# A decoder layer on one core: the second group's feed-forward tokens turned by the DMA queue

## What is computed

```python
def reference(x, ctx_2048, mask_BxS2_bk0, ...):
    x = x + _L0_attn_ref(_layernorm(x, axis=-1), ...)
    x = x + _L0_xattn_ref(_layernorm(x, axis=-1), ctx_2048, mask_BxS2_bk0)
    x = x + _L0_ffn_ref(_layernorm(x, axis=-1), ...)
    return x

def _quantized_matmul(x, w, scale):
    wq = w.astype(jnp.float8_e4m3fn).astype(x.dtype)
    return jnp.einsum('bsi,io->bso', x, wq) * scale

# feed-forward: gate = silu(q(x, gate_w)); up = q(x, up_w); q(gate * up, down_w)
```

## Time and profile before

| | us |
|---|---|
| median of 3 runs | 546.43 (546.37 to 546.47) |
| the profiled execution | 546.76 |
| its span, first to last instruction | 545.0 |

### The profile page before, as it was taken

How to read it: one execution, slowest core, us unless ns; L and a number is a source line. 1 busy time by engine, 2 the same in 40 slices (tenths; PEclk the granted TensorE clock), 3 DMA queues, 4 the chain that set the end, 5 groups by cost and what they waited for, 6 DMA issues and landing times.

```text
span 545.0 us, 10146 instructions
## 1 busy us (share of the span) xinstructions
PE 538.2 (99%) x3936; PEld 424.2 (78%) x3936; DVE 375.1 (69%) x717; ACT 283.1 (52%) x510; POOL 290.3 (53%) x262
## 2 busy tenths in 40 slices
PE   8999999999999999999999999999999999999997
PEld 7877888878888888888888888766686667866676
DVE  6999886888665886659898987355944668344422
ACT  5857886977767786776653442034501344023310
POOL 5398798985783657877795348034400343013320
PEclk9999999999999999999999999999999999999999
DMA  8951222273215310239563712100071001600001
GB/s 291 342 212 65 77 81 78 79 228 123 75 44 161 111 59 2 79 109 299 187 238 101 266 32 103 41 1 0 0 155 38 1 0 27 149 20 0 1 20 59
DMA packets 56176, 53.91 MB, mean 99 GB/s; under 512 B 15168, under 2 KB 37952, under 8 KB 56128
## 3 DMA queue, kind: packets, MB, share of 16 engines
q1 hardware_dynamic: 56128, 53.25, 31.0%
HBM read 36.46 MB, written 13.63 MB: 92 GB/s over the span
## 4 chain that ended last, share of the span: by engine, by line
PE 82%; POOL 10%; DVE 5%; issue 2%; ACT 0%; POOLq 0%; DVEq 0%
PE bank L312 33%; PE bank L506 24%; PE bank L526 15%; POOL q_w L828 2%; POOL q_w L826 2%; POOL probs L819 2%; POOL x_res L842 2%; PE bank L307 2%; PE bank L440 2%; PE bank L450 1%; PE bank L409 1%; DVE q_m L1363 1%; PE bank L361 1%; PE bank L537 1%; PE bank L556 1%
## 5 line engine op out<-in xcount | busy, mean ns | idle before, releaser
L312 PE MATMUL bank<-reduced 128*128 128x512 f32 x936 | 223.3, 394 | 0.3 <-DVE ctxT L1307 0.3
L312 PEld LDWEIGHTS bank<-reduced 128*128 128x128 f32 x936 | 172.8, 188 | 38.2 <-issue 1.1
L934 POOL TENSOR_TENSOR f_parts<-fused,f_parts 128x512 fp32r<-128x512 f32 x48 | 62.9, 1310 | 154.3 <-ACT f_parts L1206 154.3
L1188 ACT ACTIVATE tanh_g<-bank,half_gate 128x512 f32<-128x512 f32 x48 | 33.0, 687 | 141.8 <-PE bank L506 133.0
L526 PE MATMUL bank<-reduced,f_parts 128*128 128x512 f32 x360 | 83.5, 392 | 0.0
L526 PEld LDWEIGHTS bank<-reduced,f_parts 128*128 128x128 f32 x360 | 67.4, 188 | 14.2
L506 PE MATMUL bank<-reduced 128*128 128x512 f32 x288 | 72.1, 402 | 0.0
L1552 DVE SCALAR_TENSOR_TENSOR silu<-tanh_g,bank 128x512 f32<-128x512 f32 x48 | 32.9, 685 | 56.8 <-ACT tanh_g L1188 56.8
L506 PEld LDWEIGHTS bank<-reduced 128*128 128x128 f32 x288 | 54.1, 188 | 12.9
L826 POOL TENSOR_TENSOR q_w<-q_w,q_m 128x512 f32<-128x512 f32 x36 | 49.7, 1381 | 7.8 <-DVE q_m L1365 7.8
L819 POOL TENSOR_SCALAR_AFFINE_SELECT probs<-probs 128x1024 f32<-128x1024 f32 x32 | 37.0, 1161 | 31.0 <-ACT probs L1001 31.0
(11 more groups left out here) (135 smaller groups left out, 761.9 us busy)
## 6 DMA issues: line engine op xcount, KB each, us to landing
quantized<-q_w SPq DMA_DIRECT2D x36, 256.0 KB, 3.4
reduced<-quantized SPq DMA_DIRECT2D x12, 512.0 KB, 6.8
memT_sb<-in_memT SPq DMA_DIRECT2D x16, 256.0 KB, 4.9
mem_sb<-in_mem SPq DMA_DIRECT2D x16, 256.0 KB, 5.9
out<-y_sb SPq DMA_DIRECT2D x15, 256.0 KB, 2.1
q_w<-in_gate_w SPq DMA_DIRECT2D x12, 256.0 KB, 3.5
q_w<-in_up_w SPq DMA_DIRECT2D x12, 256.0 KB, 3.2
x_res<-in_x SPq DMA_DIRECT2D x3, 1024.0 KB, 8.9
```

What stands on the lines that cost most here:

```text
L312: ins = pe.matmul(dst, stationary, moving, start=(n == 0), stop=(n == len(pairs) - 1))
L934: pool.tensor_tensor(f_lo[:, f, :], fused[:, f % 2, :], f_hi[:, f, :].bitcast(F32), ALU.subtract).then_inc(f_lo_ready, 1)
```

## The change

Group 1 now goes the way of groups 2 and 3. `turn_x3`, `x3_high` and `x3_low` are gone. The planes of group 1 lie where `tanh_g` and `silu2` lie, which become one tile `gate_parts`; so the first plane waits until the last `fuse` of group 0 is done with them, and `gate(1, 0)` waits until the planes are turned. On SP the four token tiles of group 1 are turned first, each as soon as it is made, and the planes after them, all in front of the store of token 0; for groups 2 and 3 the planes stay first. `gate_up` waits for `x16` in front of the first half and for `cT_lo` only in front of the low half. In the lists of ACT and DVE the new steps stand around the last cross attention steps.

```diff
+            gate_parts = sb("gate_parts", [P, 4 * TG], F32, ffn)
+            tanh_g = gate_parts[:, 0:2 * TG].rearrange("p (n s) -> p n s", n=2)
+            silu2 = gate_parts[:, 2 * TG:].rearrange("p (n s) -> p n s", n=2)
...
             def gate_up(g, f, banks):
-                if f == 0:
+                if f == 0 and g == 0:
                     for i in range(GT):
-                        if g < 2:
-                            wait_drained(pe, ("N", G, i) if g == 0 else ("T3", g, i))
-                    if g >= 2:
-                        pe.wait_ge(x16_turned, 16 * GT * (g - 1))
-                        pe.wait_ge(x3_lo_made, GT * (g - 1))
+                        wait_drained(pe, ("N", G, i))
+                if f == 0 and g:
+                    pe.wait_ge(x16_turned, 16 * GT * g)
...
                 for n, high in enumerate((f % 2 == 0, f % 2 == 1)):
+                    if f == 0 and not high:
+                        pe.wait_ge(x3_lo_made, GT * g)
...
                     cross(G - 1, 6)
-                    for i in range(GT):
-                        turn_x3(1, i, (4, 3, 1, 7)[i])
                     down(0, 0, 0, DOWN_FIRST)
...
-            def turn_tokens(g):
-
-                sp.wait_ge(last_plane_made, GT * (g - 1))
+            def turn_planes(g):
+                sp.wait_ge(last_plane_made, GT * g)
                 sp.dma_start_transpose(out=planes_T.rearrange("p (n s) -> p n s", s=S),
                                        in_=planes(g).rearrange("p i w d -> p (i w d)")).then_inc(planes_turned, 16)
-                sp.wait_ge(x16_tok_made, GT * (g - 1))
+
+            def turn_tokens(g):
+
+                if g > 1:
+                    turn_planes(g)
                 wait_filled(sp, ("U", g - 1, FT - 1))
                 for i in range(GT):
+                    sp.wait_ge(x16_tok_made, GT * (g - 1) + i + 1)
                     sp.dma_start_transpose(out=x16[:, :, i * S:(i + 1) * S], in_=x16_tok[:, i, :]).then_inc(x16_turned, 16)
+                if g == 1:
+                    turn_planes(g)
 
             for t in range(B - 1):
-                if t in (GT, 2 * GT):
+                if t in (0, GT, 2 * GT):
                     turn_tokens(t // GT + 1)
...
             def gate(g, f):
                 src = wait_filled(act, ("G", g, f))
+                if (g, f) == (1, 0):
+                    act.wait_ge(planes_turned, 16)
...
             cross_second(*step[FT - 1])
+            for i in range(2):
+                token_high(1, i)
             cross(G - 1, 5)
-            x3_high(1)
+            for i in range(2, GT):
+                token_high(1, i)
+            for i in range(GT):
+                token_plane(1, i)
...
             cross(G - 1, 5)
+            for i in range(GT):
+                token_rest(1, i)
             cross(G - 1, 6)
-            x3_low(1)
-            y_out(0)
+            for i in range(GT):
+                token_last_plane(1, i)
+            y_out(0, range(2))
+            planes_low(1)
+            y_out(0, range(2, GT))
```

More of the change, by code:

```diff
@@ L191, in build @@
         with ffn:
-            tanh_g = sb("tanh_g", [P, 2, TG], F32, ffn)
-            silu2 = sb("silu2", [P, 2, TG], F32, ffn)
+            gate_parts = sb("gate_parts", [P, 4 * TG], F32, ffn)
+            tanh_g = gate_parts[:, 0:2 * TG].rearrange("p (n s) -> p n s", n=2)
+            silu2 = gate_parts[:, 2 * TG:].rearrange("p (n s) -> p n s", n=2)
             fused = sb("fused", [P, 2, TG], F32, ffn)
@@ L204, in planes @@
         def planes(g):
-            return x_res[:, GT * (g - 2):GT * (g - 1), :].rearrange("p i d -> p (i d)").bitcast(BF16)\
-                .rearrange("p (i w d) -> p i w d", i=GT, w=2)
+            place = gate_parts[:] if g == 1 else x_res[:, GT * (g - 2):GT * (g - 1), :].rearrange("p i d -> p (i d)")
+            return place.bitcast(BF16).rearrange("p (i w d) -> p i w d", i=GT, w=2)
         planes_T = xn2[:].rearrange("p i d -> p (i d)").bitcast(BF16)
@@ L247, in build @@
         down_loaded, down_late_loaded, down_c_loaded = sem("down_loaded"), sem("down_late_loaded"), sem("down_c_loaded")
-        x3_hi_ready, tanh_ready, f_hi_ready, f_lo_ready = (
-            sem("x3_hi_ready"), sem("tanh_ready"), sem("f_hi_ready"), sem("f_lo_ready"))
+        tanh_ready, f_hi_ready, f_lo_ready = sem("tanh_ready"), sem("f_hi_ready"), sem("f_lo_ready")
         w16_made = sem("w16_made")
@@ L508, in gate_up @@
                             ins.then_inc(done, 1)
[L510 to L513, removed]
             def down(g, i, b, first=0, last=FT):
@@ L1163, in _ @@
                     flag_slabs(slabs_at(FLAGGED, g, 3))
[L1165 to L1169, removed]
             def token_high(g, i):
@@ L1174, in token_high @@
                     wait_filled(act, ("WO", G - 1, GT - 1))
-                    if g > 2:
-                        act.wait_ge(x16_turned, 16 * GT * (g - 2))
+                    if g > 1:
+                        act.wait_ge(x16_turned, 16 * GT * (g - 1))
                 act.activation(x16_tok[:, i, :], xn2[:, i, :], ACT.Copy).then_inc(x16_tok_made, 1)
             def token_plane(g, i):
-                act.wait_ge(rest_made, GT * (g - 2) + i + 1)
-                if i == 0:
+                act.wait_ge(rest_made, GT * (g - 1) + i + 1)
+                if i == 0 and g == 1:
+                    wait_drained(act, ("U", 0, FT - 1))
+                elif i == 0:
                     act.wait_ge(y_ready, GT * (g - 1))
@@ L1520, in _ @@
                     prepare_slabs(slabs[1:])
[L1522 to L1528, removed]
             def token_rest(g, i):
-                dve.wait_ge(x16_tok_made, GT * (g - 2) + i + 1)
+                dve.wait_ge(x16_tok_made, GT * (g - 1) + i + 1)
                 dve.tensor_tensor(xn2[:, i, :], xn2[:, i, :], x16_tok[:, i, :], ALU.subtract).then_inc(rest_made, 1)
             def token_last_plane(g, i):
-                dve.wait_ge(plane_made, GT * (g - 2) + i + 1)
+                dve.wait_ge(plane_made, GT * (g - 1) + i + 1)
                 dve.tensor_tensor(planes(g)[:, i, 1], xn2[:, i, :], planes(g)[:, i, 0], ALU.subtract)\
@@ L1540, in planes_low @@
             def planes_low(g):
-                dve.wait_ge(planes_turned, 16 * (g - 1))
+                dve.wait_ge(planes_turned, 16 * g)
                 turned_planes = planes_T.rearrange("p (i w k s) -> p i w k s", i=GT, w=2, k=KT)
```

## The result

The change makes the kernel slower by 0.34%: 548.77 us (median of 12, 547.30 to 549.88) against 546.58 (12, 546.37 to 546.92), a ratio of 1.0034 (of the means; that of the medians is 1.0040) with an interval of 1.0026 to 1.0041. The forecast was 546.1 in a range of 545.0 to 547.7; the time lies outside it, on the side to which 0.13 had been given.

What follows compares the result with a forecast made beforehand. PE, busy 99% of the span, was taken to bound the kernel. Removed transposes (-1.32 us) plus a stand at cT_lo (+1.0) gave -0.3 from 546.43: 546.1 us, range 545.0 to 547.7.

Steps and rivals of the forecast that it cites:

- the side to which 0.13 had been given: The outcome that the changed kernel is slower by over 0.2% (1.1 us), chance 0.13.
- The gain: Sixteen token transposes of group 1 leave PE, so all behind them on PE moves up by 1.32 us.
- Token planes: x16 of group 1, made by ACT and turned by DMA: landed by 332.9 us, 13 us early, cost nothing.
- down weights: Late half lands at 331.1, PE wants it at 331.92; rival with token transposes in front: 546.9 or 549.5 us, chance 0.08.
- stores: Output stores of tokens 0 and 1, behind the planes' transpose on SP: landed by 347.7, needed at 349, cost nothing.
- casts: POOL's weight casts slip by about 4 us, from 341.0 to 345, before PE needs w_rest: cost nothing.
- Steps 1 to 3: On DVE: four rests, then cross(G-1, 6), then four last planes beside POOL's casts, ending at 339.4 us.
- The turns on the port: DVE's last planes and POOL's casts alternate on SBUF access: three turns of 1.45 to 1.5 us after the first plane.
- My bound of 337.9: Early bound for the end of DVE's four last planes, if all are unhindered behind the first: 337.9 us.
- Step 4: The planes' DMA transpose is issued within 0.05 us of the last plane and lands 6.8 to 6.9 us later, at 346.3.
- The delay of the low half: PE stands about 1.0 us for cT_lo, ready at 348.9 and wanted at 348.07.
- the slower one: Rival: four last planes on DVE at 1.78 us each end at 341.4, PE stands 2.9 us; 548.0 us, chance 0.09.

## Why the prediction was wrong

**The gain** of 1.32 us was right: 1.37 from the profile, and 1.4 and 1.5 in the two runs with held casts, where no stand eats it.

**Token planes, down weights, stores, casts:** as forecast, nothing. The token transposes landed 3.2 to 6.3 us after issue and not 2.5, the last at 333.2 us, which is still 13 us early. The down weights landed 7.9 us after issue, at 331.3, and PE took them at 331.58 without an idle time before the row. That rival came within 0.3 us of being true: with the token transposes issued behind it, the load took 0.5 us longer than in the earlier trace rows.

**Steps 1 to 3, up to the last plane,** were right in their sum and their mechanism. Forecast 339.4, less the 0.34 by which this execution is ahead, is 339.06; measured 338.93. The turns on the port are real: 5.14 us for four, and 2.49 for the same four once POOL is silent. The first plane took 0.81 us and the others followed at 1.44, so the turn of 1.44 that I had read from the earlier trace rows was right to the hundredth and my 1.45 to 1.5 hardly dear. `x_w` took 0.80 for 0.60. My bound of 337.9 for planes that nothing hinders was too high: at 2.49 us for four they would end at 336.7. That changes nothing, since all ends before 338.5 give the same time.

**Step 4 failed.** I took the landing of the planes' transpose as 6.8 to 6.9 us, from two cases in one program, and gave no range to it. It was 8.3. What set it is a fetch of 16384 bytes of PE's own instructions at the end of the transpose: fifteen of the sixteen completion marks were there by 345.71 us, and the wait ended with the last, at 347.28. Where the fetch lies moves with the number of instructions that PE has run, and the change itself takes 16 matmuls and 16 weight loads off that stream. This is shown: with 44 waits more on PE the landing is 6.7 us, the stand 0.26 us and the time **545.95 us**. With the 1.5 us of the late landing put in, my sum would have read -1.3 + 2.5 = +1.2; measured at the full clock +0.9.

That 545.95 lies within 0.2 us of the forecast of 546.1 is in part luck. The kernel before took 546.75 us beside it, not the 546.43 that I summed on, so the gain without the late landing is 0.8 us, not 0.3. The delay of the low half was 0.61 us (348.56 - 346.40 - 1.55), where I had 1.0: the landing was 0.2 us shorter than my 6.85, the planes' transpose was issued 0.1 earlier, and the two wake-ups of 0.1 us were nearly nothing.

The Trainium skill ("Runtime: NRT & Kernel Launch", Instruction fetch mechanics) says that the sequencer fetches its program by its own DMA queue in blocks of 16 KiB, 256 instructions, and that this is mostly hidden. The trace agrees on the block (16384 bytes on the instruction queue); it was not hidden here, though no idle time of PE in the rows above is put down to its own fetch: it was a data transfer that paid.

**Left out: the clock.** I priced each microsecond of stand at one microsecond and took the granted clock as fixed at full, because the trace of before had no gap that could tell otherwise. This term alone carries the time out of my range: the executions at the full clock have a median of 547.5 us, which the range of up to 547.7 still holds, on its wrong side. In about half of all executions of the changed kernel (12 of 22) the mean clock was 0.996 or 0.997 and the time some 1.5 us longer. With the stand filled (0.28 us) or nearly gone (0.26), none of 20 was; with 4.95 us of stand, all four were, and there the trace shows the fall inside the stand. In the changed kernel itself the fall was not caught by a profile: both of its profiled executions had a clock of 1.000. That it sits at this place there too is inferred from these runs, and how long the stand was in an execution with the low clock is not known. The kernel before, without any stand, had two low clocks in the 51 executions beside the experiments, but of another kind, 0.949 and 0.950 (550.35 and 549.96 us); none was at 0.996 or 0.997. What lowered those is not known.

Of the rivals, the slower one was right on the sign and wrong on the mechanism: the port cost what I had taken for it, not more.

## What to carry to other kernels

When a PE step is replaced by a longer chain through other engines, price what is left of the cover, not the mean: a wait that ends 1 us late in the sum can end over 2 us late through a thing that is in no list, here PE's own instruction fetch on one of the sixteen DMA engines. Before adding DVE instructions with two SBUF inputs, look at what POOL does in that stretch; moving POOL's work behind them by one wait gave the whole gain here (545.3 us), though the transpose then also ended before the fetch came. The additions had 0.95 us to spare there, less than the 1.6 us by which such a fetch can hold a landing, so that margin is not safe. And a short stand of PE can cost more than its length, since the clock was lower in half of the executions that had one; so leave PE work in reserve next to a wait that is not sure.

## What the runs showed of the hardware

- A fetch of 16384 bytes on the instruction queue, started 5.9 to 6.4 us after the issue of a 1 MB transpose, went with a landing of 8.2 to 8.5 us in all eleven cases, and one started after 3.1 us with 7.4. Started within 0.85 us of the issue (as at 340.1 us, in the kernel with sixteen idle transposes), or not at all, it left the landing at 6.7 to 6.9 in all seventeen.
- 44 fulfilled waits on PE moved that fetch from 345.7 us to 337.3, 8.4 us, more than the 5 us that I worked out from the spacing of matmuls. Why is open.
- DVE and POOL took turns where both had instructions with SBUF inputs queued: the planes followed one another at 1.44 us beside casts, at 0.6 without (2.49 us for four).
- PE's granted clock fell to 1.2 GHz during a stand of 4.95 us, and matmuls of 128x512 then took 628 ns. After stands of 1.8 to 2.0 us the mean clock was low in 12 of 22 executions, after 0.3 us in none of 20.
